# The gate's eight columns behind the weights of expert 1 in a mixture of attention projections

## The reference

```python
n1 = layernorm(x) * ln1_w + ln1_b                                  # 256 channels a token
logits = normalize(n1) @ normalize(sim, 0) - sigmoid(gates)        # 256 x 8
mask = logits > 0, and the two best experts of a token where none is
rw = softmax(relu(logits) where mask, over the 8 experts)
q = einsum('btc,ech,bte->bth', n1, q_proj, rw)                     # k and v likewise: 8 experts of 256 x 128 each
attn = softmax(causal(q @ k.T / sqrt(128))) @ v
attn_out = einsum('bth,ehc,bte->btc', attn, o_proj, rw)            # 8 experts of 128 x 256
hs = x + attn_out
```

## Time and profile before

| | before |
|---|---|
| median of 3 runs | 3219.37 us (3218.48 to 3221.39) |
| the profiled execution's own time | 3219.33 us |
| its span, first to last instruction | 3217.5 us |
| TensorE busy over the span | 2992.2 us (93%) |
| VectorE, ScalarE, GpSimd busy | 2399.8 (75%), 1857.5 (58%), 1479.9 (46%) us |
| mean granted TensorE clock | 0.962 of full speed |

### The profile page before, as it was taken

One profiled execution on the slowest core, in us unless ns is written; L12 is line 12 of the kernel. 1 busy time (PEld: TensorE's weight loads), 2 busy tenths in 40 slices (PEclk: granted clock), 3 DMA queues, 4 the chain that ended last, 5 costly groups with the idle time before them and its releaser, 6 DMA issues. The chain is left out here.

```text
span 3217.5 us, 85960 instructions
## 1 busy us (share of the span) xinstructions
PE 2992.2 (93%) x26992; PEld 2611.5 (81%) x26992; DVE 2399.8 (75%) x6465; ACT 1857.5 (58%) x6803; POOL 1479.9 (46%) x1682
## 2 busy tenths in 40 slices
PE   2999999959999999999699999999979999997978
PEld 2777777749999999998699999999967777775856
DVE  5888888856667776775677777777768888886644
ACT  2777777745555555555344444444457777776634
POOL 1454454436666666665322222222225455453555
PEclk9999999979999999999799999999989999999579
DMA  5000000010000000000100000000010000000244
GB/s 205 15 17 13 13 16 13 4 53 11 10 11 10 10 11 11 10 10 12 35 11 10 13 10 10 10 13 10 1 47 17 13 16 13 13 13 4 77 137 142
DMA packets 55912, 85.92 MB, mean 27 GB/s; under 512 B 6784, under 2 KB 42625, under 8 KB 55042
## 3 DMA queue, kind: packets, MB, share of 16 engines
q1 hardware_dynamic: 47204, 65.65, 6.7%
q0 software_dynamic: 6528, 16.92, 1.4%
q10 hardware_dynamic: 2080, 2.10, 0.2%
HBM read 57.21 MB, written 28.48 MB: 27 GB/s over the span
## 5 line engine op out<-in xcount | busy, mean ns | idle before, releaser
L538 ACT ACTIVATE L_probs<-bank,L_neg_max 128x128 f32<-128x128 f32 x2048 | 722.0, 390 | 262.9 <-DVE L_neg_max L615 262.9
L538 ACT ACTIVATION_READ_ACCUMULATOR L_probs<-bank,L_neg_max 128x1 f32 x2048 | 470.0, 229 | 0.0
L621 DVE COPY L_probsT<-bank 128x512 f32<-128x512 f32 x512 | 351.8, 687 | 123.4 <-PE bank L444 120.3
L1507 ACT ACTIVATE M_inter<-bank 128x512 f32<-128x512 f32 x256 | 153.3, 599 | 437.2 <-PE bank L69 384.5
L67 PE MATMUL bank<-W_hi,M_nT_hi 128*128 128x384 f32 x1024 | 368.7, 360 | 0.3 <-DVE M_qkv L1218 0.3
L615 DVE TENSOR_REDUCE L_neg_max<-bank 128x4 f32<-128x512 f32 x512 | 327.9, 681 | 29.1 <-PE bank L435 29.1
L68 PE MATMUL bank<-W_hi,M_nT_lo 128*128 128x384 f32 x1024 | 348.0, 340 | 0.0
L69 PE MATMUL bank<-W_lo,M_nT_hi 128*128 128x384 f32 x1024 | 347.2, 339 | 0.0
L444 PE MATMUL bank<-constants,L_probs 128*128 128x128 f32 x2048 | 330.7, 284 | 13.3 <-ACT L_probs L538 7.2
L1555 DVE TENSOR_TENSOR M_inter_lo<-M_inter,M_inter_hi 128x512 fp32r<-128x512 f32 x256 | 208.1, 813 | 173.8 <-ACT M_inter_hi L1508 163.1
L67 PE MATMUL bank<-W_hi,M_inter_hi 128*128 128x256 f32 x1024 | 290.3, 284 | 7.0 <-DVE M_inter_lo L1555 6.6
(11 more groups left out here) (309 smaller groups left out, 9394.5 us busy)
## 6 DMA issues: line engine op xcount, KB each, us to landing
L_ctx_in<-in_ctx SPq DMA_DIRECT2D x64, 256.0 KB, 2.6
M_tile<-M_sorted SPq DMA_DIRECT2D x72, 130.0 KB, 2.6
raw_weights<-in_weights SPq DMA_DIRECT2D x2, 4096.0 KB, 14.0
hs<-M_hs SPq DMA_DIRECT2D x64, 128.0 KB, 1.7
M_hs<-hs SPq DMA_DIRECT2D x32, 256.0 KB, 2.7
x_all<-in_x SPq DMA_DIRECT2D x6, 1024.0 KB, 8.2
M_sorted<-M_fill SPq DMA_DIRECT2D x16, 130.0 KB, 2.3
x_all<-in_x ACTq DMA_DIRECT2D x2, 1024.0 KB, 15.0
```

Of the source, the lines that this page charges most:

```text
L538: last = act.activation(probs[:, k % 2, i, :], score_bank[u][:, i, :], ACT.Exp, bias=neg_max[:, u, i:i + 1], scale=-1.0, accum_out=sums[:, ...
L621: dve.tensor_copy(probsT[:, k % 2], pT_ps).then_inc(pT_ready, 1)
L1507: act.activation(inter[:, e % 2], up_bank[e % 2], ACT.Gelu).then_inc(M.inter_ready, 1)
```

## The change

The eight columns of the gate are stored behind the 384 of expert 1 (high and low parts), which makes its product 392 columns wide. That product is taken out of the round of odd experts: it is made two sequences ahead, in the slot where expert 3 stood, into a bank of its own (bank 3), and serves the gate and expert 1 both. Expert 3 moves to slot 0. The gate's own product, its split columns and one of VectorE's steps (`partial`) go. The turned probabilities move from bank 3 to bank 2. `row_max` now stands ahead of `gate_first` on VectorE, `exps` ahead of `gate_exp` and expert 3's weighing ahead of the output's on ScalarE. The MLP mixture keeps its gate as it was.

```diff
+    ORDER = (3, 0, 1, 2, 5, 4, 7, 6)
...
+        first_bank, dots_ps = S.bank[3][:, 0:Q3 + E], S.bank[3][:, Q3:Q3 + E]
...
-        pT_ps = S.bank[3][:, 0:P]
+        pT_ps = S.bank[2][:, P:2 * P]
...
     # TensorE
-                def dot_gate(s, b):
+                def project_first(s, b):
                     pe.wait_ge(M.nlo_ready, s + 1)
-                    gate_products(pe, dots_ps, ..., G.split).then_inc(M.dots_made, 1)
+                    wait(pe, M.first_read, s)
+                    wait(pe, M.gate_step, T.steps * (s - 1) + T.logit_made)
+                    for k in range(KT):
+                        last = mm3(pe, first_bank, ..., [w[1][:, k, :] for w in (W.hi, W.lo)], k == 0, k == KT - 1)
+                    last.then_inc(M.first_made, 1)
...
                     for e in range(E):
-                        if one:
-                            project(s + 1, 1 - b, e ^ 1)
+                        if e == 2:
+                            if two:
+                                project_first(s + 2, b)
+                        elif one:
+                            project(s + 1, 1 - b, ORDER[e])
...
-                        if e == 1 and two:
-                            dot_gate(s + 2, b)
...
-                for s in range(2):
-                    turn_n(s, s)
-                    dot_gate(s, s)
+                turn_n(0, 0)
+                project_first(0, 0)
+                turn_n(1, 1)
                 for e in range(E):
-                    project(0, 0, e ^ 1)
+                    if e == 2:
+                        project_first(1, 1)
+                    else:
+                        project(0, 0, ORDER[e])
...
     # ScalarE
                         weigh_odd(s + 1, 1 - b, 1)
+                        weigh_odd(s + 1, 1 - b, 3)
                     if not first:
                         weigh_out(s - 1, 1 - b, 1)
                     keep_qk(s)
-                    if one:
-                        weigh_odd(s + 1, 1 - b, 3)
+                    exps(s)
                     if two:
                         gate_exp(s + 2)
-                    exps(s)
...
     # VectorE
-    for i in each:
-        last = stt(T.partial[:, i, :], dots[:, i, E:2 * E], T.rnorm[:, i:i + 1], G.gates[:], ALU.mult, ALU.subtract)
-    then(last)
-    for i in each:
-        last = stt(T.logit[:, i, :], dots[:, i, 0:E], T.rnorm[:, i:i + 1], T.partial[:, i, :], ALU.mult, ALU.add)
+        for i in each:
+            last = stt(T.logit[:, i, :], dots[:, i, :], T.rnorm[:, i:i + 1], G.gates[:], ALU.mult, ALU.subtract)
...
                         weigh_even(s + 1, 1 - b, 0)
+                    row_max(s)
                     if two:
                         gate_first(s + 2)
-                    row_max(s)
...
     # weights
-                prepare(nc, S, "W1", [(W.hi[:, e], ...) for e in range(E)] + [(W.o_hi[:, e:e + 4], ...) for e in (0, 4)], norms=2)
+                prepare(nc, S, "W1", [(W.hi[e][:, :, 0:Q3], ...) for e in range(E)]
+                        + [(*gate_columns, attention_gate.sim)] + [(W.o_hi[:, e:e + 4], ...) for e in (0, 4)], norms=2)
```

More of the change, by code:

```diff
@@ L798, in _, with gate_tiles @@
             act.activation(G.gates[:], G.gates[:], ACT.Exp, scale=-1.0).then_inc(root, 1)
-GATE_LOGIT, GATE_BEFORE, GATE_STEPS = 2, 6, 11
-def gate_tiles(sb, n):
+def gate_tiles(sb, n, summed):
+    more = 0 if summed else 1
+    count = {"summed": summed, "logit_made": 1 + more, "half": 5 + more, "steps": 10 + more}
     one = {f: sb(f"gate_{f}", [P, n]) for f in ("square_sum", "squared", "rnorm", "none", "total")}
     all_ = {f: sb(f"gate_{f}", [P, n, E]) for f in ("partial", "logit", "best", "tied", "above", "key", "order", "active", "exp")}
-    return named(n=n, **one, **all_)
+    return named(n=n, **count, **one, **all_)
 def gate_products(pe, out, left, columns):
@@ L818, in gate_products, with gate_chain @@
     return last
-def gate_chain(dve, step, index, at):
+def gate_chain(dve, T, step, index, at):
     n = [at]
@@ L827, in then @@
         ins.then_inc(step, 1)
-        dve.wait_ge(step, GATE_STEPS * index + n[0])
+        dve.wait_ge(step, T.steps * index + n[0])
     return then
 def gate_before(S, dve, T, G, dots, step, index):
-    then = gate_chain(dve, step, index, 0)
+    then = gate_chain(dve, T, step, index, 0)
     each = range(T.n)
     ts, stt = dve.tensor_scalar, dve.scalar_tensor_tensor
-    for i in each:
-        last = stt(T.partial[:, i, :], dots[:, i, E:2 * E], T.rnorm[:, i:i + 1], G.gates[:], ALU.mult, ALU.subtract)
-    then(last)
-    for i in each:
-        last = stt(T.logit[:, i, :], dots[:, i, 0:E], T.rnorm[:, i:i + 1], T.partial[:, i, :], ALU.mult, ALU.add)
+    if T.summed:
+        for i in each:
+            last = stt(T.logit[:, i, :], dots[:, i, :], T.rnorm[:, i:i + 1], G.gates[:], ALU.mult, ALU.subtract)
+    else:
+        for i in each:
+            last = stt(T.partial[:, i, :], dots[:, i, E:2 * E], T.rnorm[:, i:i + 1], G.gates[:], ALU.mult, ALU.subtract)
+        then(last)
+        for i in each:
+            last = stt(T.logit[:, i, :], dots[:, i, 0:E], T.rnorm[:, i:i + 1], T.partial[:, i, :], ALU.mult, ALU.add)
     then(last)
@@ L865, in gate_after @@
 def gate_after(dve, T, out, exp_done, step, index, ready):
-    then = gate_chain(dve, step, index, GATE_BEFORE)
+    then = gate_chain(dve, T, step, index, T.half)
     each = range(T.n)
@@ L971, in turn_n @@
                     pe.wait_ge(M.n_ready, s + 1)
-                    wait(pe, M.gate_step, GATE_STEPS * (s - 1) + 2)
+                    wait(pe, M.nlo_ready, s)
                     for k in range(KT):
@@ L975, in turn_n @@
                     last.then_inc(M.tn_ready, 1)
-                def dot_gate(s, b):
+                def project_first(s, b):
                     pe.wait_ge(M.nlo_ready, s + 1)
-                    gate_products(pe, dots_ps, [[t[:, b, k, :] for k in range(KT)] for t in nT], G.split
-                                  ).then_inc(M.dots_made, 1)
+                    wait(pe, M.first_read, s)
+                    wait(pe, M.gate_step, T.steps * (s - 1) + T.logit_made)
+                    for k in range(KT):
+                        last = mm3(pe, first_bank, [t[:, b, k, :] for t in nT], [w[1][:, k, :] for w in (W.hi, W.lo)],
+                                   k == 0, k == KT - 1)
+                    last.then_inc(M.first_made, 1)
                 def project(s, b, e):
@@ L986, in project @@
                     else:
-                        wait(pe, M.odd_read, 4 * s + e // 2)
+                        wait(pe, M.odd_read, 3 * s + e // 2 - 1)
                     for k in range(KT):
                         last = mm3(pe, q_bank[e % 2], [t[:, b, k, :] for t in nT],
-                                   [w[:, e, k, :] for w in (W.hi, W.lo)], k == 0, k == KT - 1)
+                                   [w[e][:, k, :] for w in (W.hi, W.lo)], k == 0, k == KT - 1)
                     last.then_inc((M.q_even_made, M.q_odd_made)[e % 2], 1)
@@ L1174, in _ @@
                 norm(1, 1)
-                for s in range(2):
-                    round_n(s, s)
-                    squares(s, s)
-                    gate_exp(s)
+                round_n(0, 0)
+                squares(0, 0)
+                gate_exp(0)
+                round_n(1, 1)
+                squares(1, 1)
+                weigh_odd(0, 0, 1)
+                gate_exp(1)
                 norm(2, 0)
-                for e in range(1, E, 2):
+                for e in range(3, E, 2):
                     weigh_odd(0, 0, e)
@@ L1198, in gate_first @@
                 def gate_first(s):
-                    dve.wait_ge(M.dots_made, s + 1)
+                    dve.wait_ge(M.first_made, s + 1)
                     dve.wait_ge(M.rooted, s + 1)
@@ L1203, in gate_last @@
                 def gate_last(s, b):
-                    wait(dve, M.odd_read, 4 * (s - 1))
+                    wait(dve, M.odd_read, 3 * (s - 1))
                     wait(dve, M.kept, s - 1)
@@ L1310, in root @@
                     pool.wait_ge(M.guarded, s + 1)
-                    wait(pool, M.gate_step, GATE_STEPS * (s - 1) + 2)
+                    wait(pool, M.gate_step, T.steps * (s - 1) + T.logit_made)
                     pool.tensor_tensor(T.rnorm[:], T.squared[:], S.minus_half[:, 0:T.n], ALU.pow).then_inc(M.rooted, 1)
@@ L1442, in dot_gate @@
                     pe.wait_ge(M.nlo_ready, p + 1)
-                    wait(pe, M.gate_step, GATE_STEPS * (p - 1) + 2)
+                    wait(pe, M.gate_step, T.steps * (p - 1) + T.logit_made)
                     for s in range(2):
@@ L2153, in program @@
                 W = Named()
-                W.hi, W.lo = weights(own, "W1", [P, E, KT, 3 * HID])
+                Q3 = 3 * HID
+                flat = weights(own, "W1", [P, E * KT * Q3 + KT * E])
+                ends = np.cumsum([KT * (Q3 + (E if e == 1 else 0)) for e in range(E)])
```

(2 more changed lines are left out.)

50 lines of the change are left out of this document (27 added, 23 removed).

## The result

| | before | after |
|---|---|---|
| median of the runs, us | 3218.93 (3217.53 to 3221.39, 4 runs) | 3198.64 (3196.78 to 3201.08, 4 runs) |
| the profiled execution's own time, us | 3219.33 | 3197.63 |
| its span, us | 3217.5 | 3195.7 |
| mean granted clock of TensorE | 0.962 | 0.962 |

The ratio after to before is 0.9937, with a 95% interval of 0.9919 to 0.9954. The time is 20.3 us shorter; 19.1 us were forecast, and the forecast time was 3200.2.

What follows compares the result with a forecast made beforehand. TensorE was taken to bound the steps. Terms: -26.0 small matmuls, +3.7 stall, +2.2 start, +1.4 preparation, -0.4 end, together -19.1 us from 3219.33: 3200.2 us. Own range 3195 to 3206, chance 0.66; 8 of 10: 3193 to 3214.

Steps and rivals of the forecast that it cites:

- TensorE sets the steps, so what it sheds is gained: In the stage's steps TensorE is busy 596.00 of 596.00 us, so time it sheds is gained unless another chain becomes longer.
- Four small matmuls 0.44, columns added 0.02: Per step, TensorE sheds 0.44 us of gate matmuls and takes on 0.022 for wider ones: net 0.42, 26.0 over 62 steps.
- VectorE's chain 3.81 against 3.75: From scores to slot 5, VectorE's work up to expert 2's weighing and release sums to 3.81 us; TensorE leaves it 3.75.
- 0.06 us a step for the stall: TensorE's wait at slot 5 for expert 2's weighing: 0.06 us a step, 3.7 in 62 steps; bounds 0 and 0.25 a step.
- The step in all: Each step with a gate: 0.42 us gained less 0.06 of stall; -26.0 + 3.7 us over 62 steps.
- The start +2.2: At the stage's start the first even weighing stands behind sequence 1's gate and slot 3 waits: +2.2 us, bounds 0 and 4.3.
- The preparation +1.4: Before the stage, half the output weights go from VectorE to GpSimd, 2.4 us replacing 1.17: +1.4 us, between -1.2 and +2.4.
- VectorE's chain as the main cost: Rival: in the steps, VectorE's chain sets the time, costing 0.25 us a step, 15.5 in all: 3212.0 us; chance 0.22.
- GpSimd in the gate's first half: Rival: GpSimd's work holds a gate operation half a microsecond each step, stalling TensorE 0.55: 3230 us, slower; chance 0.08.
- Hidden matmuls: Rival: the gate's small matmuls cost only their 48 columns, 0.022 us a step, so no gain: 3222 us; chance 0.02.
- a free change of order: Rival, the low end: the new order in the steps brings no stall, and the start is cheap: 3193 us; chance 0.02.
- TensorE's busy time falls below 100%: Sign: the prediction is wrong if TensorE's busy time by stretch falls more than 1% below its 100%.

Runs made afterwards that it cites:

- the cost of the gate doubled: The gate's four matmuls issued twice in each sequence, in the kernel before: 3251.13 us, ratio 1.0102 to the kernel before.
- one place further: In the changed kernel, the gate's first half moved behind expert 2's weighing, its exponential moved accordingly: 3254.68 us, ratio 1.0115 to the kernel before.
- the kernel with the order alone: Kernel before with only row maximum ahead of the gate's first half and exponentials accordingly; gate's product stays: 3239.14 us, ratio 1.0059.
- the kernel with the preparation's new order: Changed kernel with the small piece of gate columns between the two halves of the output weights: ratio 0.9934 to the kernel before.

## Why the prediction was right, by its own steps

- **TensorE sets the steps, so what it sheds is gained.** Right. With the cost of the gate doubled it came out in full.
- **Four small matmuls 0.44, columns added 0.02.** Right: 0.45 gone, 0.178 a matmul at 392 columns against 0.176 at 384. Over 55 steps the six matmuls of the slot take 1.155 us at either width, so the added columns cost even less than 0.02. The estimate of 0.10 us for four doesn't hold here, by the removal and by the doubling. But the prediction made more of it than the Trainium skill says ("TensorE: Matmul & The Clock Gate", section "Back-to-back issue gap"): the row of 60 cycles is the gap of an isolated matmul, and the same section says that at small widths it under-counts where each matmul has its own weight load. The figure for loading weights in the same page's section "LDWEIGHTS (loading the stationary operand)", about 107 ns for 128 columns, agrees with the 0.11. That the load is what sets it is not shown: no run keeps the small matmuls and leaves out their loads.
- **VectorE's chain 3.81 against 3.75.** The sum came out (3.85), the parts didn't. From the row maximum to the gate's first operation it took 0.21, not the 0.38 that the earlier trace rows have to the output. From there to the output it took 1.63, not 1.40: the output now stands idle 0.33 us behind `M_gate_order`, where a row maximum stood between the two before. Two errors of 0.2 with opposite signs: that the sum held is luck.
- **0.06 us a step for the stall.** Too small: taking the order back gained 0.11 a step, 6.6 us in all instead of 3.7. The stall itself was 0.09, the mean over 55 steps; the other 0.03 stands in the six matmuls behind it, and whether it belongs to the wait is open, since before they took 1.14 without one. It stays below the 0.25 that was the upper end; that end was what a single step of the gate adds, and putting one back did just that.
- **The step in all.** Forecast -0.36, measured -0.40. With a larger stall than forecast it should rather have been less. Over 55 steps, part by part: 0.45 less for the small matmuls, 0.09 more for the wait, and 0.04 less spread over the other matmuls, which nothing in the prediction accounts for. In the old order the step is 0.51 shorter than before where the small matmuls explain 0.43, so there it is some 0.08 us a step, 5 us; most slots were 0.01 shorter and slot 5 was 0.02. Its cause is open. It hid the mis-sized stall: the balance came out better than its terms.
- **The start +2.2.** Measured +1.5, within 0.8 to 3.3, but its terms were too large. TensorE waits 3.87 us for the first weighing and goes on at 703.72. The whole stage begins 1.6 us later, so this is 702.1 counted as the forecast was, where 703.0 was forecast: the 2.5 us allowed for the lower clock ahead of the pause were too many. Behind the pause the clock fell again:

```profile
703.72 0.44 PE L67 MATMUL bank<-W_hi,M_nT_hi 128*128 128x384 f32 x1 [3.87 <-DVE M_qkv L1236]
704.00 0.34 PE L68 MATMUL bank<-W_hi,M_nT_lo 128*128 128x384 f32 x1
...
705.27 0.52 PE L68 MATMUL bank<-W_hi,M_nT_lo 128*128 128x384 f32 x1
705.59 0.52 PE L69 MATMUL bank<-W_lo,M_nT_hi 128*128 128x384 f32 x1
```

  0.32 from matmul to matmul instead of 0.176, and 0.68 as the granted clock of 703 to 708. So of the two variants in the prediction the later one happened, with 710.8 for the third turning, yet measured it is 710.59 - 1.6 = 709.0 in the same count. The lower level lasted for ten matmuls, and the five experts took 6.9 us instead of 5.3: it cost 1.6 us, not 2.5. The 2.2 that was taken lay between the variants and came out near for that reason.
- **The preparation +1.4.** Right, with its reason. TensorE's pause ahead of the stage is 23.59 against 22.20, 1.39 more. GpSimd's piece of 1024 columns took 2.83 us, not 2.4, and the piece of VectorE beside it was held until it ended.
- **Rivals.** VectorE's chain as the main cost is refuted (0.11, not 0.25), but one operation of 0.25 away from being true. GpSimd in the gate's first half: not there, though shown to be real one place further. It is there in the second half, more than before (the three operations that are held, L875, L879 and L883, take 1.59 us together, and before, as L871, L875 and L879, 1.22):

```profile
1015.66 0.74 POOL L1358 TENSOR_TENSOR M_hs_odd<-M_hs_odd,M_out_part 128x256 f32<-128x256 f32 x1 [0.16 <-POOL M_hs_odd L1358]
1015.77 0.65 DVE L879 SCALAR_TENSOR_TENSOR M_gate_exp<-M_gate_exp,M_gate_active 128x8 f32<-128x8 f32 x1
```

  It costs nothing there, because slot 7's turning finds its input in time (L1026 follows without a wait). Hidden matmuls and a free change of order are refuted. The low end's +0.1 can't be made of the prediction's own terms: with no delay at the start, preparation and end as forecast give +1.0, so 3194 us.
- **One of the signs named was blind.** "TensorE's busy time falls below 100%" can't show a stall like this: in the kernel with the order alone, a stall of 0.34 us a step (some 15 us in this stretch) left the busy time at

```profile
804.00:1400.00 596.00, 591.75 (x3347) 549.51 (x3346) 408.50 (x1500) 322.84 (x951) 387.58 (x495) 1.00 0.03 10
```

  4 us short, 0.7% and so under the 1% that was named. In that kernel's rows above, L1008 counts as busy for 0.27 of the 0.39 us to slot 5: a matmul's modelled end reaches into the wait behind it.

## What to carry to other kernels

Take the cost of a small matmul from the starts of its neighbours, not from its columns. Where another product loads the same operand into TensorE anyway (here the turned tokens), columns that are added to that product are nearly free: 0.45 us a step became less than 0.02. When work that TensorE waits for is reordered, add up the other engine's chain from the last thing that TensorE hands over to the buffer that it needs back, and compare with TensorE's own distance; with a tie, keep what can start earlier ahead of what has to wait. And measure steps from start to start: busy time hides waits of some tenths of a microsecond.

## What the runs showed of the hardware that was not expected

- A matmul of 8 columns costs as much as one of 16, 0.11 us from start to start, eight in a row too.
- Some of VectorE's operations on 8 columns go from 0.17 to 0.53, 0.65 and 0.94 us beside GpSimd, and end with GpSimd's operation. In these traces it is those that read two tiles in SBUF (L862, L877, L879, and L875 and L883 with a scalar per token). Those with one such input (L855, L861, L880, L881: MAX8, reduction, reciprocal) and those that read a PSUM bank (L845, L1236, L1255) keep their times beside GpSimd, in every step.
- One chip took 1% longer than another for the same kernel (3250.98 against 3218.4 us), and not everywhere. The steps of the stage are the same on both. From the stage's last turning to the end it is 1728.5 us after and 1758.4 in the kernel with the preparation's new order on the other chip, and 26 of these 30 us fall behind 2952 us, in the routed expert layer. Why is open.
